# Spectral stage of a fused decoder layer: different transform rows made once, other orders by transfers inside SBUF, exponential in eight ScalarE operations

## The reference

```
x = x + attn(norm(x))        # 4-bit weights with block scales and low-rank adapters, gated feed-forward
x = x + xattn(norm(x), ctx)  # the spectral stage: the change lies here
x = x + ffn(norm(x))         # top-1 routing over 8 low-rank experts
```

```
corr = ifft(fft(q) * conj(fft(k))).real          # 64 lags per channel
w, idx = top_k(corr, 8); w = softmax(w)
out[pos] = sum_i w_i * v[min(idx_i + pos, 63)]   # no wrap: beyond the end the last value repeats
```

## Time and profile before

| | us |
|---|---|
| median of 3 runs | 832.15 (828.73 to 832.5) |
| profiled execution, first to last instruction | 830.1 |
| PE busy | 791.7 |
| DVE busy | 574.7 |
| ACT busy | 406.5 |
| POOL busy | 242.7 |

### The profile page before, as it was taken

One profiled execution on the slowest core, in us unless ns is written; L12 is line 12 of the kernel. 1 busy time (PEld: TensorE's weight loads), 2 busy tenths in 40 slices (PEclk: granted clock), 3 DMA queues, 4 the chain that ended last, 5 costly groups with the idle time before them and its releaser, 6 DMA issues. The chain is left out here.

```text
span 830.1 us, 10669 instructions
## 1 busy us (share of the span) xinstructions
PE 791.7 (95%) x3512; PEld 558.2 (67%) x3512; DVE 574.7 (69%) x1291; ACT 406.5 (49%) x647; POOL 242.7 (29%) x196
## 2 busy tenths in 40 slices
PE   3979999999999999999999999999998999999995
PEld 1335768778788888888888888887764535544542
DVE  5998775576997377386566657723458898888883
ACT  7784753564764454355255344411333445445541
POOL 0001211033453433342343333221213333233231
PEclk9999999999999999999999999999998999999997
DMA  7373210012232022022113102020000101111101
GB/s 215 132 254 126 77 38 1 1 51 69 96 103 90 13 93 85 13 89 76 39 39 97 69 18 72 13 74 1 13 14 13 39 26 51 52 29 49 38 27 39
DMA packets 25655, 50.57 MB, mean 61 GB/s; under 512 B 3264, under 2 KB 3648, under 8 KB 25600
## 3 DMA queue, kind: packets, MB, share of 16 engines
q1 hardware_dynamic: 25600, 49.89, 18.4%
HBM read 45.68 MB, written 4.19 MB: 60 GB/s over the span
## 5 line engine op out<-in xcount | busy, mean ns | idle before, releaser
L673 PE MATMUL ps<-x_hi,w_hi 128*128 128x512 f32 x448 | 176.0, 393 | 0.2 <-POOL w_lo L530 0.2
L675 PE MATMUL ps<-x_hi,w_lo 128*128 128x512 f32 x448 | 174.7, 390 | 0.0
L674 PE MATMUL ps<-x_lo,w_hi 128*128 128x512 f32 x448 | 174.3, 389 | 0.0
L789 POOL TENSOR_TENSOR h_lo<-hf,h_hi 128x512 fp32r<-128x512 f32 x56 | 74.0, 1321 | 243.2 <-ACT h_hi L784 243.2
L798 DVE TENSOR_TENSOR acc<-acc,ps 128x512 f32<-128x512 f32 x112 | 76.5, 685 | 74.9 <-PE ps L675 74.9
L673 PEld LDWEIGHTS ps<-x_hi,w_hi 128*128 128x128 f32 x448 | 84.1, 188 | 21.0 <-issue 3.3
L777 DVE TENSOR_TENSOR hf<-hf,ps 128x512 f32<-128x512 f32 x56 | 38.5, 687 | 85.5 <-PE ps L675 85.5
L675 PEld LDWEIGHTS ps<-x_hi,w_lo 128*128 128x128 f32 x448 | 84.1, 188 | 17.9
L674 PEld LDWEIGHTS ps<-x_lo,w_hi 128*128 128x128 f32 x448 | 84.2, 188 | 17.2
L530 POOL TENSOR_TENSOR w_lo<-wt,w_hi 128x512 fp32r<-128x512 f32 x42 | 62.3, 1484 | 113.8 <-ACT w_hi L523 113.8
L673 PE MATMUL ps<-w_hi,h_hi 128*128 128x512 f32 x224 | 88.2, 394 | 1.5 <-DVE acc L724 1.4
(11 more groups left out here) (151 smaller groups left out, 1381.8 us busy)
## 6 DMA issues: line engine op xcount, KB each, us to landing
codes_sb<-in_codes SPq DMA_DIRECT2D x40, 256.0 KB, 3.1
scale_sb<-in_scale_rows SPq DMA_DIRECT2D x80, 128.0 KB, 2.9
lft<-in_lora_ft SPq DMA_DIRECT2D x14, 512.0 KB, 4.4
acc<-in_x SPq DMA_DIRECT2D x4, 1024.0 KB, 8.5
ctx<-in_ctx SPq DMA_DIRECT2D x16, 256.0 KB, 2.9
out<-fin SPq DMA_DIRECT2D x16, 256.0 KB, 3.1
codes_sb<-in_codes SPq DMA_DIRECT2D x5, 512.0 KB, 3.4
codes_odd<-in_codes SPq DMA_DIRECT2D x4, 512.0 KB, 5.1
```

Of the source, the lines that this page charges most:

```text
L673: nc.tensor.matmul(bank, hi, rhs_hi, start=start, stop=False)
L674: nc.tensor.matmul(bank, hi, rhs_lo, start=False, stop=False)
L675: return nc.tensor.matmul(bank, lo, rhs_hi, start=False, stop=stop)
L789: nc.gpsimd.tensor_tensor(h_lo[:, c % 2, i], hf[:, i], h_hi[:, c % 2, i].bitcast(F32), ALU.subtract).then_inc(hlo_done, 1)
```

## The change

The transform rows are put in another order. Integer frequencies 0 to 31 and half-integer frequencies are stacked as blocks of 32 rows: real, half-integer real, imaginary, half-integer imaginary, with the Nyquist row in the place of the imaginary part of frequency 0. One transform of ctx (`pe_ku`) gives the tile ku with all different rows, one of the weights (`pe_w`) gives wu. What the products need in another order is made by six transfers from SBUF to SBUF on SP's queue (`sp_spread`): kc repeats the integer blocks for the correlation, kx has the two halves exchanged. Then pc = wu * ku on DVE (`dve_same`) and pn = wu * kx on POOL (`pool_cross`), with new output matrices OUT_S and OUT_X.

`dve_less` and its tile cd are gone: DVE negates the eight maxima (ntop), and ACT makes the exponential of corr from PSUM in eight operations of 64 columns, with ntop as the bias. For that, corr of the next tile waits for exp, and exp waits for mark.

ku is made two tiles ahead of its slot (ring of 5, kx ring of 4, ctx loaded four ahead). The users of the KW and MISC banks wait by lists (`wide`, `misc`) that follow PE's order. In the last weight group PE makes ku of tiles 0, 1 and 2 (at c = 1, 2, 3); the transforms of tile 1 between its last matmuls go, except q.

```diff
-SPEC, KCYC, KNEG, WNEG_M, INV, OUT, OUT_N = range(7)
+SPEC, KU, WU, INV, OUT_S, OUT_X = range(6)
...
+    f, odd = np.arange(L // 2), np.arange(L // 2) + 0.5
+    imag[0] = nyquist
...
+    for k, rows in ((SPEC, (real, imag, real, imag)), (KU, (k_real, neg_real @ less_last, imag, neg_imag @ less_last)),
+                    (WU, (real, neg_real, imag, neg_imag))):
+        mats[:L, k] = mats[L:, k] = np.vstack(rows).T
...
+    BLOCK = slice(0, QB // 2), slice(QB // 2, QB), slice(QB, QB + QB // 2), slice(QB + QB // 2, P)
+    HALVES = slice(0, QB), slice(QB, P)
+    def sp_spread(sp, t, b):
+        r = t % KX
+        sp.wait_ge(ku_copied, t + 1)
+        if real(t - 1):
+            sp.wait_ge(prod, t - 1)
+        for to, of in enumerate((0, 0, 2, 2)):
+            sp.dma_start(kc[BLOCK[to], b], ku[BLOCK[of], t % KU_RING]).then_inc(kc_in[b], 16)
+        if t >= KX:
+            sp.wait_ge(pcross, 2 * (t - KX) + 2)
+        for to in range(2):
+            sp.dma_start(kx[HALVES[to], r], ku[HALVES[1 - to], t % KU_RING]).then_inc(kx_in[r], 16)
...
+    wide = [(FORWARD, 0), (FORWARD, 1), (FORWARD, 2), (FIRST_Q, 0)]
+    for v in range(TT + 4):
+        wide += [(BACKWARD, v - 2)] * (0 <= v - 2 < TT) + [(FORWARD, v + 2)] * (3 <= v + 2 < TT)
...
+    def act_ku(act, t):
+        act.wait_ge(ku_ready, t + 1)
+        if t >= KU_RING:
+            n = t - KU_RING
+            act.wait_ge(psame, n + 1)
+            act.wait_ge(kx_in[n % KX], 32 * (n // KX) + 32)
+        nc.scalar.copy(ku[:, t % KU_RING], pair(KW)).then_inc(ku_copied, 1)
     def dve_product(dve, t, b):
-        dve.wait_ge(kc_copied, t + 1)
+        dve.wait_ge(kc_in[b], 64 * (t // 2) + 64)
...
     (pe_corr)
-            pe.wait_ge(marked, t)
-            pe.wait_ge(less_done, t)
+            pe.wait_ge(exp_done, t)
...
-        nc.vector.tensor_tensor(rows(cd, b), corr, top[:, b, :, 0:1].to_broadcast([P, 8, L]),
-                                ALU.subtract).then_inc(less_done, 1)
+        nc.vector.tensor_scalar(ntop[:, b], top[:, b, :, 0], -1.0, None, ALU.mult).then_inc(topd_done, 1)
...
     (act_exp)
+        act.wait_ge(topd_done, 2 * t + 2)
+        act.wait_ge(marked, t + 1)
-        nc.scalar.activation(ex[:, b], cd[:, b], ACT.Exp).then_inc(exp_done, 1)
+        for r in range(8):
+            mm = nc.scalar.activation(rows(ex, b)[:, r], corr[:, r], ACT.Exp, bias=ntop[:, b, r:r + 1])
+        mm.then_inc(exp_done, 1)
...
-        by_sequence(pe, QW, SPEC, wts[:, b]).then_inc(wc_ready, 1)
-        by_sequence(pe, KW, WNEG_M, wts[:, b]).then_inc(wn_ready, 1)
+        by_sequence(pe, KW, WU, wts[:, b]).then_inc(w_ready, 1)
...
+    def dve_same(dve, t, b):
+        dve.wait_ge(w_copied, t + 1)
-        nc.vector.tensor_tensor(pc[:, b], pair(QW), kc[:, b], ALU.mult).then_inc(pcyc, 1)
+        nc.vector.tensor_tensor(pc[:, b], wu[:, b], ku[:, t % KU_RING], ALU.mult).then_inc(psame, 1)
+    def pool_cross(pool, t, b):
+        pool.wait_ge(w_copied, t + 1)
+        pool.wait_ge(kx_in[r], 32 * (t // KX) + 32)
-            nc.gpsimd.tensor_tensor(pn[:, b, s], wns[:, b, s], kn[:, b, s], ALU.mult).then_inc(pneg, 1)
+            nc.gpsimd.tensor_tensor(pn[:, b, s], wu[:, b, s], kx[:, r, s], ALU.mult).then_inc(pcross, 1)
```

More of the change, by code:

```diff
@@ L77, in spectral_matrices @@
+    cos = lambda k: np.cos(th * np.outer(k, n))
+    sin = lambda k: np.sin(th * np.outer(k, n))
+    nyquist = cos([L // 2])
+    real, imag = cos(f), -sin(f)
+    imag[0] = nyquist
+    k_real = real.copy()
+    k_real[0, L - 1] += L
     less_last = np.eye(L)
     less_last[:, L - 1] -= 1
[L79 to L97, removed]
+    neg_real, neg_imag = cos(odd), -sin(odd)
@@ new lines, in spectral_matrices @@
+    c = np.full((L // 2, 1), 2 / L)
+    c[0] = 1 / L
+    unit = (np.arange(L // 2) > 0)[:, None]
+    last = nyquist / L
+    first = lambda row, rest: np.vstack([row, rest[1:]])
+    none = np.zeros((1, L))
+    inv = np.vstack([c * cos(f), first(none, -c * sin(f)), first(none, c * sin(f)), first(last, c * cos(f))])
+    h = 1 / L
+    out_s = np.vstack([c * cos(f) / 2, h * cos(odd), first(last / 2, c * cos(f) / 2), h * cos(odd)])
+    out_x = np.vstack([first(none, -c * sin(f) / 2), -h * sin(odd), first(none, c * sin(f) / 2), h * sin(odd)])
@@ L201, in build @@
     topd = two("topd", (8, TOPK))
-    cd = two("cd")
+    ntop = two("ntop", (8,))
     ex = two("ex")
@@ L208, in build @@
     wts = two("wts")
-    wns = two("wns", (2, D))
+    wu = two("wu", (2, D))
     pc, pn = two("pc", (2, D)), two("pn", (2, D))
@@ L913, in pe_kc @@
             pe.wait_ge(folded, PER * NG)
[L914 to L935, removed]
+        wait_for_wide(pe, FORWARD, t)
+        by_sequence(pe, KW, KU, ctx[:, b]).then_inc(ku_ready, 1)
+    def act_ku(act, t):
[5 more added lines that the diff above has]
+        nc.scalar.copy(ku[:, t % KU_RING], pair(KW)).then_inc(ku_copied, 1)
     def dve_product(dve, t, b):
         dve.wait_ge(q_ready, t + 1)
-        dve.wait_ge(kc_copied, t + 1)
+        dve.wait_ge(kc_in[b], 64 * (t // 2) + 64)
         if t == 0:
@@ L1030, in dve_weigh, with wait_for_misc @@
                                        op0=ALU.is_equal, op1=ALU.mult).then_inc(weighed, 1)
+    LAGS, TURN_H, EXPERT = range(3)
+    misc = [(LAGS, 0)]
+    for v in range(TT + 4):
+        misc += [(EXPERT, v - 4)] * (0 <= v - 4 < TT) + [(TURN_H, v - 3)] * (0 <= v - 3 < TT) + [(LAGS, v - 1)] * (1 <= v - 1 < TT)
+    def wait_for_misc(pe, kind, n):
+        k = misc.index((kind, n))
+        if k > 0:
+            user, m = misc[k - 1]
+            pe.wait_ge((lag_copied, h_copied, fin_done)[user], m + 1)
     def pe_lags(pe, t, b):
         pe.wait_ge(weighed, t + 1)
-        if t == 0:
-            pass
-        elif t == 1:
-            pe.wait_ge(lag_copied, 1)
-        else:
-            pe.wait_ge(h_copied, t - 1)
+        wait_for_misc(pe, LAGS, t)
         for j in range(KT):
@@ L1258, in _ @@
                 sp_ctx(sp, t, t)
+            for t in range(3):
+                sp_spread(sp, t, t % 2)
+                sp_ctx(sp, t + 2, t % 2)
             def piece(at):
-                if a := at(0, 2):
+                if a := at(5):
+                    sp_store(sp, *a[:2])
+                if a := at(-2, 3):
+                    sp_spread(sp, *a[:2])
+                if a := at(-4, 5):
                     sp_ctx(sp, *a[:2])
-                if a := at(6):
-                    sp_store(sp, *a[:2])
-            slots(sp, piece, 6)
+            slots(sp, piece, 5)
             for b in range(2):
@@ L1593, in _ @@
             dve_top_less(dve, 0, 0)
-            dve_less(dve, 0, 0)
             dve_mark(dve, 0, 0)
```

235 lines of the change are left out of this document (103 added, 132 removed).

## The result

The changed kernel takes 823.05 us in the median (822.48 to 823.87, 4 runs) against 832.33 (828.73 to 833.76, 4 runs): a ratio of 0.9896, 95% interval 0.9874 to 0.9918. The direction is as forecast, and the time lies in the whole range (806 to 830) but outside the forecast's own (810 to 821): 9.3 us gained, 17.4 forecast. The profiled span is 821.8 us.

A forecast was written before the change was run, and what follows sets the result against it. PE bounded the old kernel, by only 1.5 us over DVE; afterwards DVE would, at 10.59 a slot. Gains 17.5 + 1.8 - 1.9 = 17.4 give span 812.7, median 815 (own range 810 to 821, whole range 806 to 830).

The forecast's parts named there:

- PE's slot 10.25, DVE's 10.09 plus collisions: Steady slot: PE falls from 12.16 to 10.25 us, DVE from 10.61 to 10.09, plus 0.50 of collisions with POOL.
- pc +0.44, wl +0.06: Steady slot, DVE: pc waits for POOL's division, +0.44 us; wl waits for POOL's first half of pn, +0.06.
- Rival 1: Steady slots: no DVE-POOL collisions, PE stays the bound at 10.25 us; 4.4 us less, some 810.5; chance 0.18.
- rival 2: Steady slots: exponentials take 3.5 us, some 11.5 a slot; 12 us more, 827; chance 0.11.
- Rival 3: Steady slots: POOL's second half of pn precedes wl, DVE waits 1.2 us more each; 830.5, no change; chance 0.12.
- Rival 4: Steady slots: PE's waits gather, its clock falls, each slot pays 3.5 us; some 855; chance 0.07.
- Transfers at nothing: SP's queue: six more transfers per tile, 2.5 us of an idle queue with over 9 us of cover, cost nothing.
- ring of exp with 0.8 us to spare: Steady slot: the loop from correlation through exp takes 9.8 us, below 10.59, so the eight exponentials are covered by 0.8.
- Slots that are not plain: 13.45 for slot 5: Slot 5: layer-norm statistics of four more tiles, 2.9 us on DVE, now paid in full: 13.45 us.
- Slot 6 as plain, 10.6: Slot 6: counted among the ten plain slots of 10.6 us, with nothing extra.
- Entry: Stage's start: wl(0) about 2 us later, correlation 1 at 623.8 as before; smaller work in slots 1 and 2 gains 1.8.
- Slots 16 and 17: Tail: last top_less to last x3 17.2 us instead of 13.6, then 15.4 to the end instead of 17.1; loss 1.9.

The follow-up runs named there:

- psum_pc_mark: Changed kernel with pc reading the weights' transform from PSUM instead of SBUF, and mark ahead of wl in DVE's order: 813.97 us, ratio 0.9807.
- no_spread: Changed kernel without the six transfers inside SBUF per tile; products read ku in its own order, so sums differ from the reference: 823.34 us (single time).
- twice_exp: Changed kernel with the eight exponentials made twice, first into a buffer nobody reads: 842.41 us (single time).
- dup_corr: Changed kernel with the 16 correlation matmuls run twice in slot 5 alone: 823.88 us (single time).
- warm_wide: Changed kernel plus unused 512-column fill matmuls where PE waits (entry, slot 5, slot 16, last turns): 818.59 us, ratio 0.9851.
- xpow: Changed kernel with POOL's power for the second statistics issued one slot earlier, ahead of the division: 822.24 us (single time).
- entry: Changed kernel with, at the stage's entry, the first exponential ahead of mark and tile 1's product ahead of the last add: 818.62 us (single time).
- psum_pc: Changed kernel with pc reading the weights' transform from its PSUM bank instead of the SBUF copy: 824.56 us (single time).
- split: Changed kernel with the statistics of the last four tiles split, two in slot 4 and the rest in slot 5: 821.83 us (single time).
- combined: Changed kernel with pc from PSUM, mark ahead of wl, the power earlier, the statistics split and the entry's order changed: 814.52 us, ratio 0.9803.
- best: Changed kernel with pc from PSUM, mark ahead of wl, statistics split over two slots, and short fill matmuls where PE waits: 816.44 us, ratio 0.9825.
- warm: Changed kernel plus short unused fill matmuls where PE waits (entry, slot 5, slots 16 to 18, last turn): 827.24 us, ratio 0.9941.

## Why the forecast was right in kind and wrong in size

The steady slot was right, and what failed is the price of everything around it: slot 5, the entry, slot 6 and the last slots. Term by term:

- *PE's slot 10.25, DVE's 10.09 plus collisions.* Right in that DVE bounds at 10.70. The agreement of 10.25 with psum_pc_mark's 10.23 is luck: there too DVE bounds, with mark moved, and PE's own work is 9.96.
- *pc +0.44, wl +0.06.* Nearly: 10.70 for 10.59. pc takes 1.69 from its start to the next in place of 1.58, as the division starts a little later than laid out. (pc's start is 0.72 behind that of the reciprocal in that layout; the 0.96 given for it counts from the start of dve_sum. The total does not use it.)
- *Rival 1 (no collisions)* and *rival 2 (eight long exponentials)* fell: the eight take 1.75 us. *Rival 3 (wl loses its turn)* was right in four slots, where its margin was gone (3, 6, 16 and, at the entry, 2): slot 3 is 0.6 over the forecast and slot 6 1.1. *Rival 4 (the clock)* did not happen in the steady slots, whose wait is 0.43.
- *Transfers at nothing, ring of exp with 0.8 us to spare.* Right (no_spread, twice_exp).
- *Slots that are not plain: 13.45 for slot 5.* This is the step that failed most: "Once, in slot 5, the turn waits 2 us for final" was put into the range with "1.5 to 4 us more", and not into the sum. PE waited 2.48 us, the clock fell to 0.50 for nearly 7 us, and the slot took 15.15, 1.70 more than the sum had. With the clock held it takes 13.55 (dup_corr; 13.56 in warm_wide), so 1.6 of the 1.70 is the clock and the rest of the slot was priced right.
- *Slot 6 as plain, 10.6.* The power of the second statistics on POOL was not priced: 11.69 (10.70 in xpow).
- *Entry.* The forecast had 1.8 us of gain in slots 1 and 2. The first x3 came 98.9 us after the constants instead of 97.3, which leaves 0.2 of it. The order there, exp behind mark and the product behind the adds, is worth 1.4 (entry). In the changed kernel PE also waits 2.34 us for the second exponential, and the clock falls after it for some 3 us; what that alone costs was not separated.
- *Slots 16 and 17.* 19.24 us in place of 17.8. The clock's fall is 0.65 of it (warm_wide); wl loses its turn in slot 16, and with the collisions gone and the clock high it is 8.94 (psum_pc_mark).

The terms: entry 1.6, slots 3 and 4 0.7, slot 5 1.7, slot 6 1.1, slot 7 0.2, slots 8 to 15 0.8, slots 16 and 17 1.4, end 0.1: 7.6 us, by which the stage's gain of 9.85 falls short of 17.4. No single rival took it; it is what the places with a special slot cost when the steady one was right. About 2.3 us of it are shown to be the clock (slots 5 and 16), 1.0 the power in slot 6 and 1.4 the order at the entry. Not settled: what the power and the clock add before the first x3, and 0.8 us of slots 16 and 17, of which wl's lost turn is likely a part. The spread of the opening loads adds up to 2 us either way to a single execution.

## What to carry to other kernels

Here the steady slot was forecast to 1% from start-to-start distances, but entry, tail and every slot with extra work have to be laid out in the same way, with what each sends on POOL's queue. When a collision is taken away, ask first what moves earlier: here pc alone made the slot longer and with mark moved 0.47 shorter. Where the matmul engine waits for more than a microsecond, some wide matmuls of no use to anybody can shorten a kernel: fills of 512 columns that fit the wait gave 4.8 us here, while fills of 64 columns, twice too long, lost 4.4.

## What the runs showed of the hardware

- A DVE product that reads PSUM for one input runs at 1.22 us beside POOL (psum_pc); with both inputs in SBUF it takes 1.78, and 1.17 in slot 3, where it starts ahead of POOL's division.
- A small operation with one SBUF input can be held too: TENSOR_SCALAR on eight numbers took 1.04 us during pn. The Trainium skill, page "SBUF — State Buffer", section "Who interferes with whom", counts `tensor_scalar` among the operations that can take the ports shared with GpSimd, if their operands meet its conditions; this row agrees.
- PE's clock went from 2.4 to 1.2 GHz (granted 1.00 to 0.50) in these places. In every run that had them: at the waits of 2.4 to 2.5 us in slot 5 and at the end. In most runs without a fill there, but not in the changed kernel, psum_pc and no_spread: after the wait of 1.9 us at the entry. In slot 16, after waits of 1.43 to 3.08 us in nine runs, but not in psum_pc_mark (1.91), split (1.43) and entry (1.44). After 1.2 to 1.3 us in slot 5 of split and combined. Once after 0.8 us of waits behind 16 matmuls of 64 columns (best, slot 7). At the entry of warm during 36 such matmuls, and at that of best just behind 16 of them, each with a wait of 0.91 us ahead. The length of a wait alone does not tell. Where a fill of 512 columns stood, the clock stayed up.
- Six transfers inside SBUF per tile, landing in 2.4 and 3.8 us, disturbed no engine (no_spread). Beside them the loads of ctx landed in 3.8 us instead of 2.8 and the stores in 3.8 instead of 2.5.
